# A graph network's 8-head attention pass: single-step softmax between window additions, next destination rows earlier, one-hots by one comparison

## The reference

```python
q = (feats @ Wq.T + bq).reshape(bs, NHEAD, HDIM).transpose(1, 0, 2)
...
sim = jnp.einsum('hed,hed->eh', qe, ke) * scale
m = jax.ops.segment_max(sim, c, num_segments=bs)
p = jnp.exp(sim - m[c])
s = jax.ops.segment_sum(p, c, num_segments=bs)
attn = p / s[c]
out_e = attn.T[..., None] * ve
...
agg = jax.ops.segment_sum(out_e, c, num_segments=bs)
return agg @ Wo.T + bo
```

## Time and profile before

| | |
|---|---|
| median of 3 runs | 7186.11 us (7186.09 to 7192.34) |
| profiled execution, its own time | 7190.02 us |
| its span | 7188.2 us |
| busy over the span | PE 65%, DVE 62%, POOL 62%, ACT 38% |
| mean granted clock of TensorE | 0.762 |

### The profile page before, as it was taken

One profiled execution on the slowest core, in us unless ns is written; L12 is line 12 of the kernel. 1 busy time (PEld: TensorE's weight loads), 2 busy tenths in 40 slices (PEclk: granted clock), 3 DMA queues, 4 the chain that ended last, 5 costly groups with the idle time before them and its releaser, 6 DMA issues.

```text
span 7188.2 us, 103666 instructions
## 1 busy us (share of the span) xinstructions
PE 4639.1 (65%) x17172; PEld 3045.8 (42%) x17173; DVE 4426.1 (62%) x11590; ACT 2761.4 (38%) x6915; POOL 4483.7 (62%) x4928
## 2 busy tenths in 40 slices
PE   3555556867777777767666666747777735555556
PEld 2433334544444444445444444534444423334333
DVE  5555554557777777775566666835556564445456
ACT  0000000546666666654555555545555550000004
POOL 5777775045555555533777777277777737777771
PEclk7777777977877778778777777867777767777776
DMA  3333334366666666655444444344444453333334
GB/s 86 105 105 105 105 105 86 110 196 196 195 199 199 196 194 195 194 141 155 130 133 132 129 130 130 54 142 130 136 131 136 130 130 106 105 105 105 105 104 90
DMA packets 499186, 962.76 MB, mean 134 GB/s; under 512 B 105402, under 2 KB 296509, under 8 KB 491615
## 3 DMA queue, kind: packets, MB, share of 16 engines
q0 software_dynamic: 240064, 696.46, 35.6%
q1 hardware_dynamic: 258749, 262.93, 11.6%
HBM read 895.74 MB, written 64.63 MB: 134 GB/s over the span
## 4 chain that ended last, share of the span: by engine, by line
PE 33%; POOL 19%; issue 19%; DVE 15%; DVEq 6%; DMA 4%; ACT 2%; ACTq 1%; POOLq 0%; SPq 0%
POOL ring L707 19%; PE bank L974 18%; DVE acc L1429 4%; PE bank L1023 3%; DVE acc L1426 2%; DMA ring<-g_t,stage 2%; PE bank L1211 2%; DVE ring L1564 1%; PE bank L1038 1%; PE bank L1039 1%; PE bank L1040 1%; DVE aux L1484 1%; PE bank L1164 1%; DVE ohc L1435 1%; DVEq L1648 1%
## 5 line engine op out<-in xcount | busy, mean ns | idle before, releaser
L974 PE MATMUL bank<-ring,ohc 128*128 128x256 f32 (+3 forms) x8800 | 3159.5, 511 | 1561.5 <-DMA ring<-xs_t,stage 422.8
L974 PEld LDWEIGHTS bank<-ring,ohc 128*128 128x128 f32 x8800 | 2034.5, 249 | 2529.8 <-issue 1013.4
L1429 DVE TENSOR_TENSOR acc<-acc,bank 128x256 f32 (+2 forms) x3520 | 1486.1, 422 | 1476.6 <-PE bank L974 1361.2
L707 POOL DMA_INDIRECT ring<-g_t,stage x1760 | 1733.9, 985 | 521.7 <-issue 466.9
L707 POOL DMA_INDIRECT ring<-kv_t,stage x880 | 885.7, 1006 | 786.4 <-PE bank L974 552.8
L707 POOL DMA_INDIRECT ring<-in_x,stage x880 | 835.5, 949 | 262.4 <-issue 257.3
L707 POOL DMA_INDIRECT ring<-xs_t,stage x880 | 834.0, 948 | 260.8 <-issue 257.4
L837 ACT ACTIVATE aux<-bank 128x512 f32<-128x512 f32 (+1 forms) x26 | 14.9, 572 | 2226.4 <-PE bank L1153 2226.4
L766 ACT ACTIVATE ohc<-iota,rel_c 128x128 f32<-128x128 f32 x1760 | 557.0, 388 | 54.0 <-PE bank L974 53.7
L809 ACT ACTIVATE cl<-cl 128x1 f32<-128x1 f32 (+3 forms) x111 | 22.5, 203 | 1284.8 <-DVE mx L1557 1284.8
L1426 DVE SCALAR_TENSOR_TENSOR acc<-acc,aux,bank 128x264 f32 x880 | 428.3, 487 | 123.4 <-DVE acc L1426 76.1
(11 more groups left out here) (286 smaller groups left out, 5161.2 us busy)
## 6 DMA issues: line engine op xcount, KB each, us to landing
aux<-relb_t SPq DMA_DIRECT2D x56, 1024.0 KB, 5.4
aux<-q_t SPq DMA_DIRECT2D x880, 64.0 KB
relx<-relb_t SPq DMA_DIRECT2D x55, 512.0 KB, 5.1
ring<-g_t,stage POOLq DMA_INDIRECT x1760, 2.8
x<-ring SPq DMA_DIRECT2D x21, 896.0 KB, 4.2
ring<-x SPq DMA_DIRECT2D x21, 896.0 KB, 9.6
mk<-mk SPq DMA_DIRECT2D x445, 32.1 KB
ring<-in_x,stage POOLq DMA_INDIRECT x880, 2.7
```

Of the source, the lines that this page charges most:

```text
L707: g_.indirect_dma_start(out=rings[L][:, slot, 0:W], out_offset=None, in_=table[L][:, :], in_offset=bass.IndirectOffsetOnAxis(ap=stage[:, s ...
L974: return mm(agp[k % AB][:, 0:width], ohc[:, hot, :], rg[:, slot, vo:vo + width], start=True, stop=True)
L1429: tt(win, win, agp[k % AGP[L]][:, 0:width], ALU.add).then_inc(p["added"], 1)
```

## The change

In pass 1 alone:
- DVE: the 16 window additions stand alone instead of in pairs. `ch1`, `ch2` and `ch3` are cut into ten functions of one or two instructions, with an addition between each two; the drains are gone, and each step waits on a semaphore that the one before it raises. The drain after the last dot product and its semaphore `s` are gone too.
- DVE makes `oht` of the next batch with one comparison of bf16 data (`compare_turned`), behind addition 8 and ahead of the first row step. ACT's `hot_turned` is left out in this pass; ACT waits for `oht` before it reads its first column.
- PE: the scores are turned over when the last dot product is done, behind sum 8 instead of sum 11. `rows_of` stands behind sum 9 (before: 13), round 0 of the next destination rows behind sum 11 (before: behind sum 15 and `cols_of`), `cols_of` behind sum 13 (before: 15). `load_places` reads the next batch's registers behind sum 7, into a second set of 16.

```diff
-    "qe", "prod", "red", "qw0", "qw1", "qw2", "qw3")})
+    "qe", "prod", "red", "qw0", "qw1", "qw2", "qw3", "fwd", "seen", "back", "most", "lim", "lim2", "car")})
...
-    hot_turned(0, 0)
+    if L > 1:
+        hot_turned(0, 0)
...
-        if feed:
+        if feed and L > 1:
             hot_turned(b + 1, (o + 1) % 2)
...
+        if L == 1:
+            act.wait_ge(p["oht"], b + 1)
...
-    def load_places(b):
-        pe.load(edos[0:G], blk_r[0:1, ds(b * G, G)])
+    def load_places(b, par):
+        at_ = 16 * par if L == 1 else 0
+        pe.load(edos[at_:at_ + G], blk_r[0:1, ds(b * G, G)])
...
-            at_ = pe.snap(edos[k], min_val=0, max_val=NT - 1) * (2 * AW)
+            at_ = pe.snap(edos[16 * par + k], min_val=0, max_val=NT - 1) * (2 * AW)
...
-            gate(pe, p["s"], b + (past(L) + 1))
             if L == 1:
+                gate(pe, p["red"], b * 4 + 4)
                 tr(m0[0:R, 0:128], sc[:, par, 0:R], ident[:, :]).then_inc(p["st"], 1)
                 return
+            gate(pe, p["s"], b + (late(L) + 1))
...
                 dest_rows(b, par, 3)
-            sums_of(4, 12)
+            sums_of(4, 8)
+            if feed:
+                load_places(nb, npar)
+            sums_of(8, 9)
             if scores:
                 turn_scores()
+            sums_of(9, 10)
+            if scores:
+                rows_of()
+            sums_of(10, 12)
+            if feed:
+                dest_rows(nb, npar, 0)
             sums_of(12, 14)
             if scores:
-                rows_of()
+                cols_of()
             sums_of(14, 16)
-            if scores:
-                cols_of()
             if feed:
-                load_places(nb)
-                dest_rows(nb, npar, 0)
                 dest_rows(nb, npar, 1)
             if scores:
                 turn_back()
...
+    def compare_turned(b, par):
+        dve.wait_ge(p["rx"], b * 16 + 16)
+        v.tensor_scalar(turned[L][par], relb[L], iota_p[:, 0:1], None, ALU.is_equal)\
+            .then_inc(p["oht"], 1)
...
+    def scan_forward(b, par, ub):
+        dve.wait_ge(p[f"mk{par}"], ub * (16 * (H + 1)) + (masks(L, par) + 16 * (H + 1)))
+        dve.wait_ge(p["st"], b + 1)
+        v.tensor_tensor_scan(out=fw[0:R, :], data0=mk[0:R, par, 0:128], data1=m0[0:R, 0:128],
+                             initial=-BIG, op0=ALU.add, op1=ALU.max).then_inc(p["fwd"], 1)
+    def scan_backward(b, par):
+        dve.wait_ge(p["fwd"], b + 1)
+        v.tensor_tensor_scan(out=mx[0:R, ::-1], data0=mk[0:R, par, 1:129][:, ::-1],
+                             data1=fw[0:R, ::-1], initial=-BIG, op0=ALU.add, op1=ALU.max)\
+            .then_inc(p["ch1"], 1)
...
+    def rows_forward(b, par):
+        dve.wait_ge(p["row"], b + 1)
+        tt(first_rows(0, HW)[:, :, 1:G], per_head(m1[0:1, hd:hd + R])[:, :, 1:G], broken(b, 1, G - 1),
+           ALU.add)
+        v.tensor_tensor_scan(out=rows[0:1, 1, 0:HW], data0=srow[0:1, par, 0:HW],
+                             data1=m1[0:1, tl:tl + HW], initial=-BIG, op0=ALU.add, op1=ALU.max)\
+            .then_inc(p["seen"], 1)
...
+    def rows_backward(b, par):
+        dve.wait_ge(p["seen"], b + 1)
+        v.tensor_tensor_scan(out=rows[0:1, 2, 0:HW][:, ::-1], data0=srow[0:1, par, 1:HW + 1][:, ::-1],
+                             data1=rows[0:1, 0, 0:HW][:, ::-1], initial=-BIG,
+                             op0=ALU.add, op1=ALU.max).then_inc(p["back"], 1)
...
+    def rows_most(b):
+        seen, back = first_rows(1, HW), first_rows(2, HW)
+        dve.wait_ge(p["back"], b + 1)
+        tt(first_rows(4, R), seen[:, :, 1:G + 1], back[:, :, 1:G + 1], ALU.max)
+        tt(first_rows(3, R)[:, :, 0:1], seen[:, :, 0:1], broken(b, 0, 1), ALU.add)\
+            .then_inc(p["most"], 1)
+    def rows_before(b):
+        most = first_rows(4, R)
+        dve.wait_ge(p["most"], b + 1)
+        tt(first_rows(3, R)[:, :, 1:G], most[:, :, 0:G - 1], broken(b, 1, G - 1), ALU.add)\
+            .then_inc(p["ch2"], 1)
+        v.tensor_copy(per_head(fprow[0:1, 0, 0:HW])[:, :, 0:1], most[:, :, G - 1:G])
...
+    def limit_before(b, par):
+        dve.wait_ge(p["col"], b + 1)
+        v.scalar_tensor_tensor(m2[0:R, :], mk[0:R, par, 129:257], m1[0:R, on - 8:on - 7], mx[0:R, :],
+                               ALU.add, ALU.max).then_inc(p["lim"], 1)
+    def limit_behind(b, par):
+        dve.wait_ge(p["lim"], b + 1)
+        v.scalar_tensor_tensor(m2[0:R, :], mk[0:R, par, 257:385], m1[0:R, on - 7:on - 6], m2[0:R, :],
+                               ALU.add, ALU.max).then_inc(p["lim2"], 1)
+    def carry(b):
+        dve.wait_ge(p["lim2"], b + 1)
+        tt(cl[0:R, 2:3], m1[0:R, on - 8:on - 7], m2[0:R, 0:1], ALU.subtract).then_inc(p["car"], 1)
+    def differences(b):
+        dve.wait_ge(p["car"], b + 1)
+        tt(dd[0:R, :], m0[0:R, 0:128], m2[0:R, :], ALU.subtract).then_inc(p["ch3"], 1)
...
+    if L == 1:
+        compare_turned(0, 0)
...
@@ -1633,29 +1724,50 @@
                 load_offsets(b, par, 0)
             weigh_four(1)
             pair(1)
-            add(0, 2)
+            add(0, 1)
             dots(1)
-            add(2, 4)
+            add(1, 2)
             weigh_four(2)
+            add(2, 3)
             pair(2)
-            add(4, 6)
+            add(3, 4)
             dots(2)
-            add(6, 8)
+            add(4, 5)
             pair(3)
-            add(8, 10)
+            add(5, 6)
             dots(3)
-            if scores:
-                dve.drain()
-                dve.sem_inc(p["s"], 1)
-            add(10, 12)
-            if scores:
-                ch1(b, par, ub)
-            add(12, 14)
-            if scores:
-                ch2(b, par)
-            add(14, 16)
-            if scores:
-                ch3(b, par)
+            add(6, 7)
+            if scores:
+                scan_forward(b, par, ub)
+            add(7, 8)
+            if scores:
+                scan_backward(b, par)
+            add(8, 9)
+            if feed:
+                compare_turned(b + 1, (o + 1) % 2)
+            if scores:
+                rows_forward(b, par)
+            add(9, 10)
+            if scores:
+                rows_backward(b, par)
+            add(10, 11)
+            if scores:
+                rows_most(b)
+            add(11, 12)
+            if scores:
+                rows_before(b)
+            add(12, 13)
+            if scores:
+                limit_before(b, par)
+            add(13, 14)
+            if scores:
+                limit_behind(b, par)
+            add(14, 15)
+            if scores:
+                carry(b)
+            add(15, 16)
+            if scores:
+                differences(b)
```

More of the change, by code:

```diff
@@ L1043, in _ @@
                         gate(pe, p["es"], L - 1)
-                    load_places(0)
+                    load_places(0, 0)
                     if L == 1:
@@ new lines, in scan_backward @@
+                    def scan_backward(b, par):
[3 more added lines that the diff above has]
+                            .then_inc(p["ch1"], 1)
+                    first_rows = lambda k, w: per_head(rows[0:1, k, 0:w])
+                    broken = lambda b, o, n: cneg_r[0:1, ds(b * G + o, n)].unsqueeze(1).to_broadcast([1, H, n])
@@ L1590, in batch @@
                         c, cset, _, cp, _ = batch_at(L, i, o - 1)
+                        feed = scores and (not isinstance(b, int) or b + 1 < NBS[L])
                         def add(k0, k1):
```

## The result

The changed kernel takes 6989.93 us (median of 4 runs, 6978.94 to 6997.19) against 7186.10 before (4 runs). The ratio is 0.9724, 95% interval 0.9708 to 0.9741: 196 us or 2.8% less. The forecast was 6991. The profiled execution took 6978.94.

A forecast was written before the change was run, and what follows sets the result against it. DVE was nearest to full, losing time to paired additions and waits in the head. Parts summed to 25.9 us a batch, plus 1.4 for PE's low clock: 27.3 against 30.92, times 54 is 195 us, so 6991; range 6900 to 7115.

The forecast's parts named there:

- Head: From the batch's last instruction to the window scaling: 2.45 us instead of 5.71, first product no longer waiting for PE.
- Middle: From the window scaling to the last dot product's end: six separate additions replace ten in pairs, 13.43 us instead of 16.37.
- scores: From the last dot product's end to the backward scan's end: transposition starts without DVE's drain, 2.03 us instead of 2.53.
- Tail: From the backward scan to the batch's last instruction: 8.0 us at PE's high clock instead of 6.08, now holding eight additions.
- The clock's fall: PE's clock fell while spacing single sums; the new middle's low clock would end inside the batch's last part, costing 1.4 us.
- Rival 2: PE's clock rises before the batch's last part, so 25.9 us a batch stand: 6915 us, chance 0.20.
- Comparison: DVE's one-hot comparison over 2048 elements takes 0.7 us, hidden in a 1.25 us wait for PE's row operands.
- ACT's lost work at nothing: Removing ACT's two passes over 2048 elements saves nothing, since nothing waited for them.
- The feed: SP's queue lands the comparison's 512 KB row 18.9 us after the batch's end, DVE wants it at 18.3; it just fits.
- rivals 4 and 5: The comparison's row lands late: 4, in 7 to 8 us, 7088 to 7142, chance 0.12; 5, in 10 us, 7250, 0.05.
- DMA share: In the attention pass, the DMA share would go from 0.66 to 0.75 with the shorter batch.
- Rival 1: Port turns: the comparison waits out a gather's instruction and takes 1.7 us instead of 0.7; 7015 us, chance 0.05.

The follow-up runs named there:

- the filled kernel before: The kernel before the change, with 12 small unread bf16 matmuls added ahead of each of sums 4 to 11: 7164.30 us, ratio 0.9952.
- the paired middle: The changed kernel with its first six window additions in three adjacent pairs again: 7050.58 us, ratio 0.9796 to the kernel before.
- the filled kernel: The changed kernel with 12 small unread bf16 matmuls added ahead of each of sums 4 to 8: 6880.28 us, ratio 0.9553 to the kernel before.
- the added comparison: The changed kernel with one more two-input bf16 comparison on DVE into unused memory, directly ahead of the real one: 7000.14 us, ratio 0.9728.
- run 53: Not a run label: 53 counts the comparisons, of 55 in the changed kernel's profiled run, that lie wholly inside a gather; that run took 6978.94 us.

## Why the prediction was right, and where it was not

- **Head**, 2.45 forecast, 2.44 measured. The number is DVE's own product and dot product, and it stands as soon as PE and ACT are ready in time. The reason given for that was in part wrong. The prediction moves round 0 ahead of sums 12 and 13 so that the first product need not wait; with round 0 back behind sum 15 the head is still 2.42 us. It counts nothing for the clock in the head, where the 24 destination rows had taken 5.1 us at 1.2 GHz; the one fully clocked head of the filled kernel before puts some 2.5 us on it. The registers read early and the additions spread over the tail let PE begin sooner; no run takes these two apart.
- **Middle**, 13.43 forecast, 13.29 measured; **scores**, 2.03 and 1.88. The adjacent additions were right, and the paired middle confirms them from the other side.
- **Tail**, 8.0 at the high clock plus 1.4 for the low one, together 9.4, measured 9.72. The sum was near by luck of two errors. At a full clock the tail is 7.30, and in it the column operands cost 0.20 + 0.26 as addition 12's wait and theirs, so DVE's part is 6.84: I had 7.3 for it and 0.7 for the column operands. The low clock costs 9.72 - 7.30 = 2.4 us and not 1.4, because it ends only some 4.5 us before the next T, when PE has already done the row operands and most of round 0 slowly. The first row step begins 1.87 us after the backward scan, in the filled kernel 1.23; I had put 1.6 for it at either clock.
- **The clock's fall.** The prediction says that the low stretch of the earlier trace rows began while PE was spacing single sums. PE's timeline puts its start, 2021.1, behind sum 15: PE had stood idle for 1.15 us in front of the column operands, had done these, and was loading places. Only the other low stretch of a batch began while sums were being spaced, in pairs. The expectation for the new middle, that single sums between additions would let it fall, came true all the same.
- **Rival 2** (PE keeps up) was given 25.9 us a batch. It did not happen; the filled kernel, with the clock nearly full, has 24.7.
- **Comparison**, 0.7 forecast from a small bf16 row, measured 747 ns at the median (728 to 971), with no wait before it and a wait of 0.83 behind it. Its hole is 0.75 + 0.83 = 1.6 us, not 1.25. The Trainium skill (VectorE: DVE Perf Modes, "The perf-mode tier table") puts a one-source bf16 instruction over 2048 elements at 693 ns and a two-source one at 1224; the second agrees with the 1.22 us of the added comparison, and the first is 54 ns short here.
- **ACT's lost work at nothing**: shown, since ACT doing it again leaves the steady period at 27.30 us.
- **The feed** was wrong too. I let the row for the comparison land 18.9 us after T and be wanted at 18.3 of the same batch, "just fits". SP's timeline of the changed kernel shows the row being issued right behind the comparison:

```profile
2010.94 0.33 SPq L480 DMA_DIRECT2D relx<-relb_t  x1
```

  The comparison of that batch ends at 2010.7 (it starts at 2009.97); the row issued here is for the comparison at 2037.31. If it lands in the 5.2 us of the earlier trace rows, it has 26 us for that, some 21 to spare. I had the gate of that load (the buffer being read) a batch off, so rivals 4 and 5 had 0.17 of the chance for nothing. It was in no term of the sum, which is why the number did not suffer.
- **DMA share** 0.75 forecast, 0.73 measured. **POOL idle** about 6 us: 3.07 + 0.91 + 2.12 = 6.1.

## What to carry to other kernels

Read the granted clock at the place where an engine waits, not its mean: here the mean was 0.80 before and 0.81 after, while the low stretch left the head and a stretch of 10 us in the tail still cost 2.4 us in each of 54 batches, and 60 small matmuls a batch that compute nothing took it away. Such a filler was worth a quarter of that in the old order, where PE stood idle once more before the critical work; put the wanted order first, then fill what gaps it leaves. When a wait goes, put the moved instruction back alone before calling it the cause. Compare steady periods, since the last two alone moved a mean by up to 0.3 us. Before calling a load late, find what frees its buffer and in which iteration.

## What the runs showed of the hardware

**A gather beside the comparison.** The comparison by line, and POOL's timeline around one that runs from 2009.97 to 2010.72, both in the changed kernel:

```profile
L1481 DVE TENSOR_SCALAR oht<-relx,iota_p x55: 728/747/971, 1498.0 to 2966.2; 128x2048 bf16<-128x2048 bf16 x55
```

```profile
2008.43 0.95 POOL L707 DMA_INDIRECT ring<-kv_t,stage  x1 [0.30 <-issue]
2009.68 1.15 POOL L707 DMA_INDIRECT ring<-kv_t,stage  x1 [0.30 <-issue]
```

The gather instruction that holds the comparison inside it takes 0.20 us longer. Of the 55 comparisons of this run 53 lie wholly inside a gather; they take 744 to 752 ns, and those gathers 1.15 us at the median, where the others have 0.95. In the filled kernel a gather begins during 43 of the 55 comparisons, and their median is 971 ns: there the comparison pays. The Trainium skill (SBUF — State Buffer, "SBUF: two separate sides") has a VectorE instruction in a two-port mode and a GpSimd instruction wait for each other on a shared port pair, the second for the whole of the first. Here the two overlap, and the price is some 0.2 us on one side or the other, though POOL's spans are rough. Rival 1, which rested on the full turn, was not seen.

**A late low stretch finds the next place.** With pairs in the middle the periods do not settle: they go round 26.9, 28.8 and 29.7 us, and the low stretch lies elsewhere in each. The changed kernel keeps 27.3 in batch after batch and the filled one 24.7 and 24.8. With 0.75 us less on DVE a batch (the one-hots on ACT) or 1.2 us more (the longer comparison) the changed kernel still has 27.24 to 27.34 from the sixth batch end to the 52nd, each with 10.24 us at the low clock. A mean period can hide this; only the single periods show it. Why one order locks and another wanders was not tried, and how far the clock and the period hold each other was not taken apart.
